# Rows per expert block raised from 224 to 256 in a mixture-of-experts tail

## The reference, cut to what matters

```
logits = xf @ router_w                      # 625 x 8
probs = jax.nn.softmax(logits, axis=-1)
topw, topi = jax.lax.top_k(probs, K)        # K = 2 of 8 experts
combine = zeros((n, E)).at[arange(n)[:, None], topi].add(topw)
h = jax.nn.silu(jnp.einsum('nd,edf->nef', xf, w1))     # w1: 8 x 1024 x 1024
ye = jnp.einsum('nef,efd->ned', h, w2)                 # w2: 8 x 1024 x 1024
routed = jnp.einsum('ne,ned->nd', combine, ye)
gu = xf @ shared_gate_up; gate, up = (gu[:, :F], gu[:, F:])
shared = jax.nn.sigmoid(xf @ shared_gate_w) * (jax.nn.silu(gate) * up @ shared_down)
return routed + shared
```

## Time and profile before

| | |
|---|---|
| median of 3 executions | 1242.14 us (1241.31 to 1242.23) |
| the profiled execution's own time | 1242.14 us |
| span of its instructions | 1240.4 us |
| mean granted TensorE clock | 0.996 of full speed |
| TensorE busy | 1216.2 us, 98% of the span |
| VectorE, ScalarE, GpSimd busy | 581.7, 457.5 and 65.4 us |

### The profile page before, as it was taken

How to read it: one execution, slowest core, us unless ns; L and a number is a source line. 1 busy time by engine, 2 the same in 40 slices (tenths; PEclk the granted TensorE clock), 3 DMA queues, 4 the chain that set the end, 5 groups by cost and what they waited for, 6 DMA issues and landing times.

```text
span 1240.4 us, 17997 instructions
## 1 busy us (share of the span) xinstructions
PE 1216.2 (98%) x7269; PEld 1047.4 (84%) x7269; DVE 581.7 (47%) x832; ACT 457.5 (37%) x581; POOL 65.4 (5%) x87
## 2 busy tenths in 40 slices
PE   6999999999999999999999999999999999999998
PEld 4677778998678898997778899989899889889886
DVE  6876676426632312222135353234454554455455
ACT  6675554322411202111022242223554555455440
POOL 2000000000000000000000015020000000000003
PEclk9999999999999999999999999999999999999999
DMA  5120004211053111135010335254666666665747
GB/s 179 53 77 18 18 18 166 89 48 69 0 204 117 69 67 69 68 130 173 1 68 1 127 96 157 76 181 179 246 213 241 211 237 221 241 209 209 262 159 258
DMA packets 78433, 162.13 MB, mean 131 GB/s; under 512 B 7238, under 2 KB 7504, under 8 KB 78379
## 3 DMA queue, kind: packets, MB, share of 16 engines
q1 hardware_dynamic: 65442, 129.86, 30.0%
q10 hardware_dynamic: 8712, 17.97, 4.0%
q0 software_dynamic: 4224, 13.55, 3.3%
HBM read 138.25 MB, written 23.10 MB: 130 GB/s over the span
## 4 chain that ended last, share of the span: by engine, by line
PE 94%; DVE 2%; ACT 2%; DVEq 1%; ACTq 0%; issue 0%; DMA 0%; SPq 0%
PE ps L1273 28%; PE ps L1275 28%; PE ps L1274 28%; PE ps L1333 7%; PE ps L1315 2%; PE ps L1378 1%; DVE w_lo L871 1%; PE ps L1410 0%; ACT w_hi L588 0%; PE ps L1362 0%; DVE src_oh L930 0%; PE ps L1387 0%; PE ps L1464 0%; DVEq L934 0%; ACT dst_oh L600 0%
## 5 line engine op out<-in xcount | busy, mean ns | idle before, releaser
L871 DVE TENSOR_TENSOR w_lo<-w_raw,w_hi 128x2048 fp32r<-128x2048 f32 x108 | 243.2, 2289 | 170.9 <-ACT w_hi L588 170.3
L588 ACT CAST w_hi<-w_raw 128x2048 fp32r<-128x2048 f32 x108 | 202.7, 1913 | 132.4 <-PE ps L1275 67.1
L1275 PE MATMUL ps<-xe_hi,w_lo 128*128 128x224 f32 x512 | 140.5, 274 | 0.0
L1274 PE MATMUL ps<-xe_lo,w_hi 128*128 128x224 f32 x512 | 140.5, 274 | 0.0
L1273 PE MATMUL ps<-xe_hi,w_hi 128*128 128x224 f32 x512 | 140.4, 274 | 0.0
L1333 PE MATMUL ps<-dst_oh,src_oh 125*128 125x314 f16 (+1 forms) x800 | 112.9, 303 | 12.1 <-ACTq L602 7.2
L1333 PEld LDWEIGHTS ps<-dst_oh,src_oh 125*128 125x128 f16 (+1 forms) x800 | 84.3, 107 | 40.5 <-DVEq L934 13.7
L1273 PE MATMUL ps<-w_hi,he_hi 128*128 128x512 f32 (+1 forms) x256 | 101.2, 395 | 0.0
L1275 PE MATMUL ps<-w_hi,he_lo 128*128 128x512 f32 (+1 forms) x256 | 100.2, 391 | 0.0
L1274 PE MATMUL ps<-w_lo,he_hi 128*128 128x512 f32 (+1 forms) x256 | 100.0, 391 | 0.0
L1273 PEld LDWEIGHTS ps<-xe_hi,w_hi 128*128 128x128 f32 x512 | 98.3, 192 | 0.5
(11 more groups left out here) (240 smaller groups left out, 2167.7 us busy)
## 6 DMA issues: line engine op xcount, KB each, us to landing
w_raw<-in_L_ffn_w SPq DMA_DIRECT2D x64, 1024.0 KB, 5.5
w_raw<-in_L_gnn_W_neigh SPq DMA_DIRECT2D x8, 1024.0 KB, 5.8
w_raw<-in_L_gnn_W_self SPq DMA_DIRECT2D x8, 1024.0 KB, 5.2
w_raw<-in_L_ffn_shared_gate_up SPq DMA_DIRECT2D x8, 1024.0 KB, 6.1
w_raw<-in_L_mix_Wv SPq DMA_DIRECT2D x4, 1024.0 KB, 8.2
w_raw<-in_L_mix_Wk SPq DMA_DIRECT2D x4, 1024.0 KB, 5.0
w_raw<-in_L_mix_Wq SPq DMA_DIRECT2D x4, 1024.0 KB, 5.4
w_raw<-in_L_mix_Wo SPq DMA_DIRECT2D x4, 1024.0 KB, 6.1
```

Source lines behind the costliest of these rows:

```text
L588: copy(w_hi[b][:, s * HK:(s + 1) * HK, :], w_raw[s][:, :, :]).then_inc(hi_done, 1)
L871: V_.tensor_tensor(w_lo[b][:, k, :], w_raw[s][:, :, :], as32(w_hi[b][:, k, :]), ALU.subtract).then_inc(lo_done, 1)
L1274: mat(out_ap, lh, rl, start=False, stop=False)
L1275: return mat(out_ap, ll, rh, start=False, stop=stop)
```

## The change

`B` becomes 256, so that a block is two full groups of 128 rows. The row groups of unequal size (`BROWS`) go, and with them the views that are cut at 96 rows: tiles, loads and stores are all 128 rows. `MAXB`, the bound on the number of blocks, falls from 14 to 13, by its formula. The list of slots is read back by one DMA in place of two, and the copy of a block's token list is one instruction on GpSimd in place of two. The diff, without the places that only drop `BROWS` again:

```diff
-    B, BS = 224, 256
-    BROWS = (128, B - 128)
-    BC = len(BROWS)
+    B = 256
+    BC = B // 128
     MAXB = X + (2 * N - X) // B + 1
-    SLOTS = MAXB * B
-    SLOTC = SLOTS // 112
-    assert SLOTC * 112 == SLOTS
+    SLOTC = MAXB * BC
...
-    y_b = y_d.rearrange("(j r) f -> r j f", r=B)
-    block_rows = lambda s: slice(s * 128, s * 128 + BROWS[s])
-    y_block = lambda j, s, f0, f1: y_b[block_rows(s), bass.ds(j, 1), f0:f1].rearrange("p c f -> p (c f)")
+    y_c = y_d.rearrange("(c p) f -> p c f", p=128)
+    y_block = lambda c, f0, f1: y_c[:, bass.ds(c, 1), f0:f1].rearrange("p c f -> p (c f)")
...
-            for s in range(BC):
-                pool.dma_start(cols[0:BROWS[s], s, :], slot_d.rearrange("(j r) o -> r (j o)", r=B)[block_rows(s), :],
-                               allow_slow_non_contiguous=True).then_inc(cols_loaded, 16)
-            pool.wait_ge(cols_loaded, 16 * BC)
+            pool.dma_start(cols[:, :], slot_d.rearrange("(c p) o -> p (c o)", p=128),
+                           allow_slow_non_contiguous=True).then_inc(cols_loaded, 16)
+            pool.wait_ge(cols_loaded, 16)
...
-                for s in range(BC):
-                    nc.gpsimd.tensor_copy(idx2[0:BROWS[s], s:s + 1], cols[0:BROWS[s], s, bass.ds(j + 1, 1)])
+                nc.gpsimd.tensor_copy(idx2[:, :], cols[:, bass.ds(j * BC + BC, BC)])
                 nc.gpsimd.drain()
                 for s in range(BC):
                     nc.gpsimd.indirect_dma_start(
-                        out=xg[0:BROWS[s], s, :], out_offset=None, in_=xn2_d,
-                        in_offset=bass.IndirectOffsetOnAxis(ap=idx2[0:BROWS[s], s:s + 1], axis=0)).then_inc(xg_loaded, 16)
+                        out=xg[:, s, :], out_offset=None, in_=xn2_d,
+                        in_offset=bass.IndirectOffsetOnAxis(ap=idx2[:, s:s + 1], axis=0)).then_inc(xg_loaded, 16)
...
-                        nc.scalar.activation(PS(key)[:, 0, 0:2 * B], PS(key)[:, 0, 0:2 * B], ACT.Silu).then_inc(silu_done, 1)
+                        nc.scalar.activation(PS(key)[:, 0, :], PS(key)[:, 0, :], ACT.Silu).then_inc(silu_done, 1)
...
                                 last = passes(PS(key)[:, 0, a * B:(a + 1) * B], (wh[:, k, w_cols], wl[:, k, w_cols]),
-                                              (xe_hi[:, k, 0:B], xe_lo[:, k, 0:B]), k == 0, k == KF - 1)
+                                              (xe_hi[:, k, :], xe_lo[:, k, :]), k == 0, k == KF - 1)
...
-                    transposes(("xe+", s, f), lambda a: xg[0:BROWS[s], s, (f * HK + a) * 128:(f * HK + a + 1) * 128],
-                               HK, BROWS[s], BROWS[s], j)
+                    transposes(("xe+", s, f), lambda a: xg[:, s, (f * HK + a) * 128:(f * HK + a + 1) * 128],
+                               HK, 128, 128, j)
...
-                        by_tokens(key, PS(key)[0:BROWS[s], 0, :], HE, J_X + h, slice(s * 128, s * 128 + BROWS[s]),
+                        by_tokens(key, PS(key)[:, 0, :], HE, J_X + h, slice(s * 128, (s + 1) * 128),
```

More of the change, by code:

```diff
@@ L219, in gps_layer @@
         t2_lo = at("t2_lo", R2 + PAIR // 2, [128, KF, TP], f32r)
[L220 to L224, removed]
+        XE = KF * B * 4
+        xe_hi = at("xe_hi", R2, [128, KF, B], f32r)
+        xe_lo = at("xe_lo", R2 + XE, [128, KF, B], f32r)
+        he_hi = at("he_hi", R2 + 2 * XE, [128, KF, B], f32r)
+        he_lo = at("he_lo", R2 + 3 * XE, [128, KF, B], f32r)
         y_s = at("y_s", R2 + 4 * XE, [128, 2, HW], f32)
@@ L291, in gps_layer @@
         wts = following("wts", [T, 3, NT], f32, 4)
-        cols = following("cols", [128, BC, MAXB], u32, 4)
+        cols = following("cols", [128, SLOTC], u32, 4)
         idx2 = following("idx2", [128, BC], u32, 4)
@@ L311, in gps_layer @@
         je = following("je", [T, MAXB], f32, 4)
-        zslot = following("zslot", [112, SLOTC], u32, 4)
+        zslot = following("zslot", [128, SLOTC], u32, 4)
         assert off[0] <= RG + RGS, (off[0], RG + RGS)
@@ L515, in _ @@
             pool.wait_ge(route_set, 1)
-            pool.dma_start(slot_d.rearrange("(p c) o -> p (c o)", p=112), zslot[:, :]).then_inc(zero_stored, 16)
+            pool.dma_start(slot_d.rearrange("(p c) o -> p (c o)", p=128), zslot[:, :]).then_inc(zero_stored, 16)
             pool.wait_ge(zero_stored, 16)
@@ L532, in _ @@
             blocks = pool.value_load(table[0:1, 1, 0:1], min_val=1, max_val=MAXB - 1)
-            for s in range(BC):
-                nc.gpsimd.tensor_copy(idx2[0:BROWS[s], s:s + 1], cols[0:BROWS[s], s, 0:1])
-            nc.gpsimd.drain().then_inc(idx_ready, 1)
+            nc.gpsimd.tensor_copy(idx2[:, :], cols[:, 0:BC]).then_inc(idx_ready, 1)
             pool.wait_ge(idx_ready, 1)
@@ L811, in _ @@
                 for f in range(2):
-                    hi_of(("xe", s, f), xe_hi[:, f * HK:(f + 1) * HK, s * 128:s * 128 + BROWS[s]],
-                          PS(("xe", s, f))[:, 0, 0:HK * BROWS[s]].rearrange("p (k t) -> p k t", t=BROWS[s]))
+                    hi_of(("xe", s, f), xe_hi[:, f * HK:(f + 1) * HK, s * 128:(s + 1) * 128],
+                          PS(("xe", s, f))[:, 0, :].rearrange("p (k t) -> p k t", t=128))
             split_hi(J_X)
@@ L820, in _ @@
             for s in range(BC):
-                act.dma_start(y_b[block_rows(s), MAXB - 1, 0:HW], zrow[0:BROWS[s], 0:HW]).then_inc(y_stored[s], 16)
-                act.dma_start(y_b[block_rows(s), MAXB - 1, HW:D], zrow[0:BROWS[s], HW:D]).then_inc(y_rows, 16)
+                act.dma_start(y_c[:, (MAXB - 1) * BC + s, 0:HW], zrow[:, 0:HW]).then_inc(y_stored[s], 16)
+                act.dma_start(y_c[:, (MAXB - 1) * BC + s, HW:D], zrow[:, HW:D]).then_inc(y_rows, 16)
             with act.Fori(blocks, MAXB - 1) as j:
                 for s in range(BC):
-                    act.dma_start(y_block(j, s, 0, D), zrow[0:BROWS[s], :]).then_inc(y_rows, 16)
+                    act.dma_start(y_block(j * BC + s, 0, D), zrow[:, :]).then_inc(y_rows, 16)
             with act.Fori(0, blocks) as j:
@@ L832, in _ @@
                         wait_unit(key, j)
-                        nc.scalar.activation(PS(key)[:, 0, 0:2 * B], PS(key)[:, 0, 0:2 * B], ACT.Silu).then_inc(silu_done, 1)
+                        nc.scalar.activation(PS(key)[:, 0, :], PS(key)[:, 0, :], ACT.Silu).then_inc(silu_done, 1)
                         act.wait_ge(silu_done, j * (KF // 2) + (n + 1))
-                        copy(he_hi[:, 2 * n:2 * n + 2, 0:B], PS(key)[:, 0, 0:2 * B].rearrange("p (k n) -> p k n", k=2)).then_inc(hi_out, 1)
+                        copy(he_hi[:, 2 * n:2 * n + 2, :].rearrange("p k n -> p (k n)"), PS(key)[:, 0, :]).then_inc(hi_out, 1)
                 def rows_hi(s, f):
-                    hi_of(("xe+", s, f), xe_hi[:, f * HK:(f + 1) * HK, s * 128:s * 128 + BROWS[s]],
-                          PS(("xe+", s, f))[:, 0, 0:HK * BROWS[s]].rearrange("p (k t) -> p k t", t=BROWS[s]), j)
+                    hi_of(("xe+", s, f), xe_hi[:, f * HK:(f + 1) * HK, s * 128:(s + 1) * 128],
+                          PS(("xe+", s, f))[:, 0, :].rearrange("p (k t) -> p k t", t=128), j)
                 for s, f in FIRST:
@@ L849, in _ @@
                         act.wait_ge(y_stored[s], j * 32 + (16 * h + 16))
-                        copy(y_s[0:BROWS[s], s, :], PS(key)[0:BROWS[s], 0, :]).then_inc(y_copied, 1)
+                        copy(y_s[:, s, :], PS(key)[:, 0, :]).then_inc(y_copied, 1)
                         act.wait_ge(y_copied, j * (2 * BC) + (h * BC + s + 1))
                         act.sem_inc(free[slot(key)], 1)
-                        act.dma_start(y_block(j, s, h * HW, (h + 1) * HW), y_s[0:BROWS[s], s, :]).then_inc(y_stored[s], 16)
+                        act.dma_start(y_block(j * BC + s, h * HW, (h + 1) * HW), y_s[:, s, :]).then_inc(y_stored[s], 16)
                         if h == s == 0:
@@ L1219, in _ @@
                 for f in range(2):
-                    transposed_lo(("xe", s, f), xe_lo, xe_hi, s, f, BROWS[s])
+                    transposed_lo(("xe", s, f), xe_lo, xe_hi, s, f, 128)
             def shared_out(h, i, base=None):
@@ L1238, in _ @@
                         key = ("he", n)
-                        two = lambda t: t[:, 2 * n:2 * n + 2, 0:B]
-                        lo_of(key, two(he_lo), PS(key)[:, 0, 0:2 * B].rearrange("p (k n) -> p k n", k=2), two(he_hi), j)
+                        two = lambda t: t[:, 2 * n:2 * n + 2, :].rearrange("p k n -> p (k n)")
+                        lo_of(key, two(he_lo), PS(key)[:, 0, :], two(he_hi), j)
                 for s, f in FIRST:
-                    transposed_lo(("xe+", s, f), xe_lo, xe_hi, s, f, BROWS[s], j)
+                    transposed_lo(("xe+", s, f), xe_lo, xe_hi, s, f, 128, j)
                 split_lo(J_X + 3, j)
                 for s, f in LATER:
-                    transposed_lo(("xe+", s, f), xe_lo, xe_hi, s, f, BROWS[s], j)
+                    transposed_lo(("xe+", s, f), xe_lo, xe_hi, s, f, 128, j)
                 split_lo(J_X + 4, j)
@@ L1551, in _ @@
                 for f in range(2):
```

(3 more changed lines are left out.)

4 lines of the change are left out of this document (2 added, 2 removed).

## The result

The changed kernel takes 1252.22 us (median of four executions, 1249.73 to 1253.54), the kernel before beside it 1241.77. The ratio of the two is 1.0078, 95% interval 1.006 to 1.0095: slower by 7.5 to 11.8 us (the quotient of the two medians, 1.0084, lies inside). The forecast was 1259.7 us, its range 1256.0 to 1264.5.

A forecast was written before the change was run, and what follows sets the result against it. TensorE was taken to bound the kernel. Added to 1242.14 us, 16.0 us for the `he` matmuls, 1.6 for transposes and 0 for the rest gave 1259.7 us, range 1256.0 to 1264.5.

The forecast's parts named there:

- What bounds the kernel: Whole kernel: TensorE, busy 1216.2 of 1240.4 us and holding 94% of the chain.
- the eight blocks: Expert loop: still 8 blocks with 256 slots, so the same number of matmuls and 64 weight loads.
- no wait takes the place of the added work: Expert blocks: TensorE never waits inside a block, so longer matmuls are paid in full.
- The `he` matmuls: First expert layer: 1536 matmuls going from 224 to 256 columns, 10.4 ns more each, 16.0 us.
- the even price between 224 and 314 columns: `he` matmuls: each column costs 0.369 ns from 224 to 314, so 32 more cost 11.8 ns.
- the line below 314 columns: `he` matmuls: 224 stands on a floor, 256 lies below 314 at 0.417 ns a column: 120.6 ns, 9.0 more.
- The transposes: Second row group in each block, 96 to 128 columns: 0.20 us more a block, 1.6 us in all.
- The `y` units: Second expert layer, 96 to 128 stationary columns: nothing counted, bounds -2.2 to +0.6 us.
- The base: Starting time for the sum: 1242.14 us, the profiled execution and the median of the runs before.
- the one at 821 us: Half clock behind transposes ahead of `sd`, 1.5 us lost; rival that wider transposes repeat or lengthen it: 1261.2 us, 6%.
- the full column price: Rival for the `he` matmuls: all 32 added columns paid, 13.3 ns each matmul, 1264.2 us, 12%.
- The load as the only bound: Rival: 256 columns still hide behind the weight load, `he` step stays, only transposes cost: 1243.7 us, 4%.

The follow-up runs named there:

- after_he224: Changed kernel with only the `he` matmuls put back to 224 streamed columns: 1240.18 us, ratio 0.9997 to the kernel before.
- the widths: Three single runs of the changed kernel, its four `he` units streaming different widths from 128 to 256 columns: 1240.52, 1242.53 and 1245.73 us.
- stationary: Kernel before with 128, 96, 64 and 32 stationary columns in the four `he` units, 224 streamed; one execution, 1228.98 us.
- the 69 executions of before: Kernel before, unedited, timed again alone and beside other runs: median 1240.74 us.
- executions with fillers: Small f16 matmuls, results never read, put around TensorE's waits: kernel before 1237.99 us, with fewer of them 1237.82; changed kernel 1251.51.

## Why the prediction was wrong, step by step

What bounds the kernel, the eight blocks, and that no wait takes the place of the added work: right, by the stretches without idle time and the 64 loads.

The `he` matmuls: the step that failed. The mechanism was right (1536 matmuls on the path, all of the cost, shown by `after_he224`), the size was not. I priced 10.4 ns each, 16.0 us, where 8.3 ns, 12.7 us, were measured, below even the low end of 9.0 that I took for a bound. The upper end of the middle that I took was the even price between 224 and 314 columns, which the widths show to be wrong: the step is flat to 240 columns and bends behind that. The lower end, the line below 314 columns, gave 120.6 ns where 119.9 was measured. I had the floor and its cause in the rows of the weight loads, and `stationary` bears it out; had I trusted it, the term would have been 13.8. The line's constant of 14.0 ns, taken from 314 columns, was treated as exact; at 256 it is 13.2, and at 248 11.7.

The transposes: 0.20 us a block forecast, 0.19 measured. The `y` units: nothing taken, -0.16 us a block measured, -1.3 us in all, inside the bound that I had given.

The base: a second step that failed. The forecast added its 17.6 us to 1242.14, an execution with three falls of the clock. I had seen the one at 821 us and put it down as a rival that could only add time; that it was already in the base, and that two others were, I had not asked. The expectations put each fall at 1.5 to 1.8 us; by the stretches of all profiles they cost 0.9 to 1.2, 1.7 and 1.5 to 1.6 us. The profile of the changed kernel has none of the three. With the median of the 69 executions of before, 1240.74, and the 13.0 us of the blocks the parts give 1253.7; the changed kernel's 12 executions have 1251.3. A part of these 2.4 us is the third fall, which went with the 128-row transposes: 33 of 69 executions against none of 28. Whether the two earlier falls came less often by chance (9 of the 28 at 1.0 against 13 of 69) these counts don't settle, and chance in the start of the first transposes adds to it.

Of the 7.5 us between the forecast of 1259.7 and the 1252.2 measured, 3.3 are the size of the `he` term, 1.3 the `y` units and 2.9 the base. Neither the first nor the last by itself would have left the range; together they did.

In sum for the profiled pair: 12.7 + 1.5 - 1.3 - 5.0 = 7.9 us, the growth of the span. Two small slips changed nothing: 5.59 us over 24 less 213.3 ns is 19.6 and not 19.7 ns, and seven blocks of 47.1 us in place of eight of 44.95 would have given some 1212 and not 1214 us.

The rivals: the full column price (13.3 ns, 1264.2 us) is refuted by the flat part of the curve. By the gap rule of the Trainium skill ("TensorE: Matmul & The Clock Gate", "Back-to-back issue gap") the difference would be those 13.3 ns; but the section gives the rule for an isolated matmul and says that in a stream of loads and matmuls both set the spacing, which the prediction left out. The trace agrees with the second: the difference is 8.3 ns, since 224 columns stood behind their weight load. The load rule of the same page ("LDWEIGHTS (loading the stationary operand)") gives 107 ns for 128 columns by estimate, and the flat part lies at 110.6 to 112.3. The load as the only bound had the right floor, but the streamed side overtakes it at about 240 columns, short of 256. The same page's "Part 1: The HAM clock gate" says that the clock's change isn't tied to the start of a kernel, so that one kernel shows different counts of slow matmuls; the groups of executions here agree as far as the two earlier falls go.

## What to carry to other kernels

Before pricing a wider or narrower streamed operand, see whether the weight load sets the step: here everything from 128 to 240 columns cost the same, so narrowing a block below 240 rows buys nothing in the `he` stage, and going past it costs. A base time has a state too: look for stretches with a lowered clock in the profile from which the sum starts, and ask how many executions share them. Small matmuls placed in waits that TensorE has anyway took 2.7 and 3.3 us off the median of this kernel (0.2% by the ratio) and most of its scatter. And a change can alter such a wait by the way, as here ahead of `sd`.

## What the runs showed of the hardware

An fp32r matmul that loads 128 new stationary columns steps no faster than about 111 ns even with only 128 columns streamed; with 96 stationary and 224 streamed columns it is 103.8 ns. At 256 streamed columns there is an extra cost: 3.1 ns for the last four columns, and 3.6 to 6.3 ns less with a narrower load. A fall of the granted clock to 1.2 GHz behind a wait of TensorE costs 0.9 to 1.2, 1.7 and 1.5 to 1.6 us at the three places, comes in some executions and not in others of the same program, and stayed away in all 30 executions with fillers. At the third place it stayed away as well in all seven profiles in which TensorE idled 1.49 in place of 1.70 us there.
